# Key-weight sums on VectorE, queries in another buffer and quantised between later pairs, in a perceiver block

## What is computed

```python
q = (x @ Wq + bq).reshape(1, B * N, H, hd)
kv = (cond @ Wkv + bkv).reshape(1, -1, 2, H, hd)
k, v = (kv[:, :, 0], kv[:, :, 1])
scale = 1.0 / np.sqrt(hd).astype(np.float32)
q = jnp.transpose(q * scale, (0, 2, 1, 3))
...
q = _fq_sym(q, axis=-1)
k = _fq_sym(k, axis=-1)
v = _fq_sym(v, axis=2)
```

## Time and profile before

| | |
|---|---|
| median of 3 executions | 2779.63 us (2777.3 to 2780.09) |
| the profiled execution's own time | 2777.66 us |
| its span, first to last instruction | 2775.9 us |
| mean granted TensorE clock | 0.963 of 2.4 GHz |
| PE, DVE, ACT, POOL busy | 91%, 75%, 41%, 32% |
| stage A | from 0 to 92.3 us |
| stage B, pair 0 | 92.33 to 144.5 us |
| stage B, pairs 1 to 31 | from 144.51 us on, 38.86 us each where TensorE never waits |

### The profile page before, as it was taken

How to read it: one execution, slowest core, us unless ns; L and a number is a source line. 1 busy time by engine, 2 the same in 40 slices (tenths; PEclk the granted TensorE clock), 3 DMA queues, 4 the chain that set the end, 5 groups by cost and what they waited for, 6 DMA issues and landing times. The chain is left out here.

```text
span 2775.9 us, 42997 instructions
## 1 busy us (share of the span) xinstructions
PE 2525.2 (91%) x16296; PEld 1284.6 (46%) x16296; DVE 2084.2 (75%) x2967; ACT 1142.4 (41%) x1096; POOL 879.4 (32%) x385
## 2 busy tenths in 40 slices
PE   6699999999999999999878888888877999999998
PEld 3244444444444444444345454545554448544443
DVE  6877877778777877778679999999966434666664
ACT  3222222222222222222379999999982124311100
POOL 0432232223322233222256556466431460101100
PEclk9899999999999999999889999999998995899999
DMA  6043344433454345433668888888863223000000
GB/s 251 15 118 103 89 113 128 114 99 90 121 128 106 93 104 128 121 102 90 164 168 184 199 202 197 208 191 202 208 156 142 91 79 60 1 16 16 1 4 31
DMA packets 557343, 321.54 MB, mean 116 GB/s; under 512 B 401968, under 2 KB 533296, under 8 KB 552368
## 3 DMA queue, kind: packets, MB, share of 16 engines
q1 hardware_dynamic: 557232, 319.91, 44.7%
HBM read 149.95 MB, written 69.21 MB: 79 GB/s over the span
## 5 line engine op out<-in xcount | busy, mean ns | idle before, releaser
L1230 DVE TENSOR_SCALAR_CACHE_REDUCE at_sc<-at_score 128x1024 f32<-128x1024 f32 x512 | 601.6, 1219 | 21.0 <-PE at_score L1109 14.6
L1328 ACT ACTIVATE at_sc<-at_sc,at_bias,at_qs 128x4096 uint16<-128x4096 f32 x128 | 485.0, 3793 | 1.1 <-DVE at_bias L1242 1.1
L631 PE MATMUL kv_vacc<-kv_whi,kv_xthi 128*128 128x512 f16 x1024 | 388.9, 380 | 17.7 <-PEq L272 17.7
L631 PE MATMUL kv_vacc<-kv_wlo,kv_xthi 128*128 128x512 f16 x1024 | 388.9, 380 | 0.0
L631 PE MATMUL kv_vacc<-kv_whi,kv_xtlo 128*128 128x512 f16 x1024 | 388.9, 380 | 0.0
L639 PE MATMUL kv_kacc<-kv_wk,q_t 128*128 128x512 f16 x1536 | 347.0, 379 | 0.0
L712 ACT ACTIVATE q_t<-q_t 128x512 f16<-128x512 f32 x128 | 77.1, 626 | 503.1 <-POOL q_t L886 311.6
L884 POOL TENSOR_TENSOR q_t<-kv_rows 128x512 f32<-128x512 f32 x32 | 41.1, 1283 | 636.2 <-DMA kv_rows<-in_ctx 606.6
L639 PE MATMUL kv_kacc<-kv_wk,kv_xthi 128*128 128x512 f16 x768 | 229.5, 381 | 11.3 <-DVE kv_xtlo L490 11.3
L809 DVE SCALAR_TENSOR_TENSOR kv_val<-kv_vacc,kv_bias 128x512 f32<-128x512 f32 x128 | 87.7, 686 | 196.9 <-PE kv_vacc L631 193.1
L639 PEld LDWEIGHTS kv_kacc<-kv_wk,q_t 128*128 128x128 f16 x1536 | 150.3, 98 | 181.2
(11 more groups left out here) (228 smaller groups left out, 4329.3 us busy)
## 6 DMA issues: line engine op xcount, KB each, us to landing
kv_rows<-in_ctx SPq DMA_DIRECT2D x64, 512.0 KB, 7.0
values<-kv_val SPq DMA_DIRECT2D x32, 1024.0 KB, 6.4
keys_turned<-o SPq DMA_DIRECT2D x32, 1024.0 KB, 5.1
at_v_raw<-values SPq DMA_DIRECT2D x16, 2048.0 KB, 8.4
at_kt<-keys_turned SPq DMA_DIRECT2D x32, 512.0 KB, 5.2
x<-keys_turned SPq DMA_DIRECT2D x31, 512.0 KB, 5.2
x<-in_x SPq DMA_DIRECT2D x2, 2048.0 KB, 8.0
kv_wk<-in_wq SPq DMA_DIRECT2D x2, 2048.0 KB, 12.7
```

The costliest lines, as they stand in the source:

```text
L631: last = nc.tensor.matmul(v_acc[2 * s + c][:], a[s][:, k, :], b[:, c, k, :], start=(k == 0 and q == 0), stop=(k == KD - 1 and q == 2))
L1230: nc.vector.tensor_scalar(sc[n % 2][:, c * SC:(c + 1) * SC], score[pos % 2][:], 1.0, None, ALU.mult, ALU.max, accum_out=part_max[n % 2][:, ...
L1328: nc.scalar.activation(prob[n % 2][e], sc[n % 2][:, e * EC:(e + 1) * EC], ACT.Exp, bias=bias[n % 2][:], scale=qs_pair[j][:, t:t + 1], accu ...
```

## The change

Four things are altered; nothing else in the program is.

- The sums of the key weights move from GpSimd to VectorE, in stage A (`sums(dve, n)`, called three times), and the first sum t1 = b12 - b11 is written to a room of its own (`val`), so b11 stays whole. The table of the seven half-panels is in another order; products name them by new numbers. High parts 0 and 1 now wait for three low parts of panels, 2 and 3 for four. The low parts of the first pair's rows and the first two key weights stand ahead of the takes of the first Wq half.
- `x` and `o` are swapped: the queries lie in `x`, the raw key weights in `o`, which is free when the eight transposes are done. The bias of the queries has a tile of its own (`q_bias`).
- ScalarE splits the first Wq panel ahead of the transposed rows (`high_first=1`).
- Pair 0 nearly has the loop's order on TensorE: value(0,0) first, then M1, M6, M5, value(0,1), M7, M4, M2, M3, value(1,0), value(1,1). The queries are quantised between pairs: `queries.vector` behind pair 1, `queries.round` behind pair 2, the two ScalarE copies behind pairs 3 and 4. SyncE waits for them only after a quarter of the pairs.

```diff
             if ahead is not None:
-                kw.load(sp, turner.rows_ready, T * (turner.norms + 1))
+                kw.load(sp, turner.turned, turner.first + len(turner.units))
...
         def _(act):
+            turner.root(act)
+            for m in splits[:high_first]:
+                panels.high(act, m)
             turner.scalar(act)
-            for m in splits:
+            for m in splits[high_first:]:
                 panels.high(act, m)
...
             if ahead is not None:
-                act.wait_ge(panels.lo_ready, len(panels.sources))
-                for m in range(4):
-                    kw.high(act, m)
+                act.wait_ge(panels.lo_ready, 3)
+                kw.high(act, 0)
+                kw.high(act, 1)
+                act.wait_ge(panels.lo_ready, 4)
+                kw.high(act, 2)
+                kw.high(act, 3)
 
...
             turner.vector(dve)
             for m in split_first:
+                if ahead is not None and m == 2:
+                    kw.sums(dve, 0)
                 panels.low(dve, m)
+            if ahead is not None:
+                kw.low(dve, 0)
+                kw.sums(dve, 1)
+                kw.low(dve, 1)
+                kw.sums(dve, 2)
+                for s in range(2):
+                    tokens.low(dve, 0, s)
...
                 if ahead is not None and n == 0:
-                    for m in range(3):
-                        kw.low(dve, m)
-                    for s in range(2):
-                        tokens.low(dve, 0, s)
+                    kw.low(dve, 2)
                     kw.low(dve, 3)
...
-            if ahead is not None:
-                kw.sums(pool)
...
         act.wait_ge(self.scaled, 7)
-        for c in range(2):
-            self.nc.scalar.activation(self.twice[:, :, :, c, :], self.q[:].rearrange("p t (h d) -> p t h d", d=HD),
-                                      ACT.Copy).then_inc(self.step, 1)
+        self.nc.scalar.activation(self.twice[:, :, :, c, :], self.q[:].rearrange("p t (h d) -> p t h d", d=HD),
+                                  ACT.Copy).then_inc(self.step, 1)
...
+    def __init__(self, chip, wk, whole, key, val, wkv):
+        self.nc, self.wkv, self.whole = chip.nc, wkv, whole
...
+        t1 = val[:].rearrange("p h s d -> p (h s d)").rearrange("p (k n) -> p k n", n=HALF)
+        self.b11, self.b21, self.b12, self.b22, self.t1 = b11, b21, b12, b22, t1
+
+        self.raw = (b22, b21, b11, t1, b22, b12, b21)
...
-    def load(self, sp, rows_ready, n):
+    def load(self, sp, turned, n):
...
-        sp.wait_ge(rows_ready, n)
+        sp.wait_ge(turned, n)
         sp.dma_start(self.whole, self.wkv[0]).then_inc(self.loaded, 16)
...
         else:
-            act.wait_ge(self.summed, n - 2)
+            act.wait_ge(self.summed, (1, 3, 2, 4)[n - 3])
         if n == 6:
-            act.wait_ge(self.lo_ready, 5)
+            act.wait_ge(self.lo_ready, 6)
...
-    def sums(self, pool):
+    def sums(self, dve, n):
...
+        if n == 0:
+            dve.wait_ge(self.loaded, 48)
+            nc.vector.tensor_tensor(self.t1, self.b12, self.b11, ALU.subtract).then_inc(done, 1)
+            dve.wait_ge(done, 1)
+            nc.vector.tensor_tensor(self.b12, self.b22, self.b12, ALU.subtract).then_inc(done, 1)
+        elif n == 1:
+            dve.wait_ge(self.lo_ready, 1)
+            nc.vector.tensor_tensor(self.b22, self.b22, self.t1, ALU.subtract).then_inc(done, 1)
+        else:
+            dve.wait_ge(self.lo_ready, 2)
+            dve.wait_ge(done, 3)
+            nc.vector.tensor_tensor(self.b21, self.b21, self.b22, ALU.subtract).then_inc(done, 1)
...
-        q_room = queries.q[:].rearrange("p t n -> p (t n)").bitcast(F16)
+        q_room = room[:].rearrange("p t n -> p (t n)").bitcast(F16)
...
             body(0, True, False)
-            sp.wait_ge(queries.step, queries.DONE)
...
                     sp.wait_ge(k_stored, 16 * (n + 1) * quarter)
+                    if n == 0:
+                        sp.wait_ge(queries.step, queries.DONE)
                     heads.keys(sp, 0, 0, (n,))
...
                 pe.wait_ge(src.lo_ready, 2 * i + 1)
...
                 if first:
                     value_sums(i, first, 0, 0)
-                    value_sums(i, first, 0, 1)
-                    pe.wait_ge(src.lo_ready, 2)
-                    value_sums(i, first, 1, 0)
-                    value_sums(i, first, 1, 1)
-                if not first:
...
+                else:
                     pe.wait_ge(k_taken, 7 * (i - 1) + C11)
-                product(0, *low_half(0), 0)
+                product(0, *low_half(0), 2)
                 if not first:
...
                 else:
-                    pe.wait_ge(kw.lo_ready, 6)
+                    pe.wait_ge(kw.lo_ready, 5)
                 pe.wait_ge(s_lo_ready, 4 * i + 1)
-                product(1, *summed_rows(S2), 5)
+                product(1, *summed_rows(S2), 4)
                 if not first:
...
                 product(2, *summed_rows(S1), 3)
-                if not first:
-                    value_sums(i, first, 0, 0)
+                value_sums(i, first, 0, 1 if first else 0)
+                if first:
+                    pe.wait_ge(kw.lo_ready, 6)
                 pe.wait_ge(k_taken, 7 * i + U2)
...
-                product(1, *summed_rows(S3), 4)
+                product(1, *summed_rows(S3), 5)
                 pe.wait_ge(src.lo_ready, 2 * i + 2)
                 if first:
                     pe.wait_ge(kw.lo_ready, 7)
...
-                product(2, *summed_rows(S4), 2)
+                product(2, *summed_rows(S4), 0)
                 if not first:
                     value_sums(i, first, 0, 1)
-                    if last:
-                        for n in range(4):
...
-                    value_sums(i, first, 1, 1)
...
+                value_sums(i, first, 1, 0)
...
+                value_sums(i, first, 1, 1)
...
-                    act.wait_ge(kw.lo_ready, 6)
+                    act.wait_ge(kw.lo_ready, 5)
                 act.wait_ge(k_summed, 7 * i + M1)
                 nc.scalar.activation(key[:, 0, left], k_acc[0][:], ACT.Copy, scale=UNSCALE).then_inc(m1_ready, 1)
+                if first:
+                    kw.high(act, 6)
...
             sums_high(0, S1, None)
+            kw.high(act, 5)
             sums_high(0, S3, None)
             sums_high(0, S4, None)
-            kw.high(act, 5)
-            queries.scalar(act)
-            kw.high(act, 6)
-            each_pair(act, body)
+            body(0, True, False)
+            for i in range(1, 5):
+                body(i, False, False)
+                if i > 2:
+                    queries.scalar(act, i - 3)
+            with act.Fori(5, LAST_PAIR) as i:
+                body(i, False, False)
+            body(LAST_PAIR, False, True)
...
                     take_value(i, 0, 0)
-                    take_value(i, 0, 1)
                 else:
                     dve.wait_ge(v_stored, 16 * i)
...
-                if not first:
-                    take_value(i, 0, 1)
+                take_value(i, 0, 1)
                 low_parts(i, 1, 1)
...
-            queries.vector(dve)
-            queries.round(dve)
             kw.low(dve, 4)
             sums_low(0, S2)
             sums_low(0, S1)
+            kw.low(dve, 5)
             sums_low(0, S3)
-            kw.low(dve, 5)
-            each_pair(dve, body)
+            body(0, True, False)
+            body(1, False, False)
+            queries.vector(dve)
+            body(2, False, False)
+            queries.round(dve)
+            with dve.Fori(3, LAST_PAIR) as i:
+                body(i, False, False)
+            body(LAST_PAIR, False, True)
...
-                q = o
+                kw = KeyWeights(chip, wk, o[:].rearrange("p t n -> p (t n)").rearrange("p (k n) -> p k n", n=HALF), key, val,
+                                a["wkv"])
+                q = x
+                q_bias = chip.sb(c, "q_bias", [P, D], F32)
...
                 project(chip, "pq", panels, 0, 2, (0, 1, 2), ((3,), ()),
-                        (q, natural, xt_hi, xt_lo, ident32, x, None, x_loaded),
-                        lambda n, t: bias[:, cols(n)], lambda n, t: q[:, t, cols(n)], ahead=(kw, tokens))
+                        (o, natural, xt_hi, xt_lo, ident32, x, None, x_loaded),
+                        lambda n, t: bias[:, cols(n)], lambda n, t: q[:, t, cols(n)], ahead=(kw, tokens), high_first=1)
```

More of the change, by code:

```diff
@@ L259, in low, with project @@
                                             op1=ALU.subtract).then_inc(self.lo_ready, 1)
[L262 removed]
+def project(chip, tag, panels, first, count, split_first, split_after, rows, addend, out, added=None, beside=None, high_first=0,
             stats=None, ahead=None):
@@ L491, in low, with keys_and_values @@
                                             op0=ALU.mult, op1=ALU.subtract).then_inc(self.lo_ready, 1)
```

(3 more changed lines are left out.)

40 lines of the change are left out of this document (12 added, 28 removed).

## The result

| | before | changed |
|---|---|---|
| median | 2778.76 us (2777.3 to 2780.09, 4 runs) | **2762.74 us** (2760.14 to 2763.46, 4 runs) |
| span of the profiled execution | 2775.9 us | 2761.6 us |
| mean granted TensorE clock | 0.963 | 0.964 |

The ratio is 0.9942, 95% interval 0.993 to 0.9955: 16 us faster. The forecast was 2767, its range 2757 to 2773. The sign and the range held, and so did the gains of stage A and pair 0. The third term, what the moved queries cost, did not: TensorE waits 6.05 us in pairs 1 to 6 where the forecast had 13.6, which is under the 9 us that the forecast had named as a sign of being wrong. A smaller error, in the clock, hid part of that, and the median is 4.3 us from the forecast.

What follows compares the result with a forecast made beforehand. TensorE bounds the kernel from pair 1 on; only the way there can shorten. 25.4 us gained less 13.6 of waits is 11.8, giving 2765.9, plus about one for the median: 2767 us, range 2757 to 2773.

Steps and rivals of the forecast that it cites:

- the gains of stage A and pair 0: Ahead of pair 1: stage B begins 13.0 us earlier, pair 1 at 120.5 rather than 145.9, 25.4 us gained.
- The third term: Pairs 2 to 6: moved query steps delay M6's take and the row load, so TensorE waits 13.6 us.
- S: Stage A: time of one 128x2048 key-weight sum on VectorE, taken as 2.2 us, between 1.22 and 4.42.
- (c): Stage A gains less, by slower sums or late raw weights (+4.4 us): 2771 us; chance 0.11.
- (e): Stage A's end is set by something other than VectorE's chain, such as TensorE's end; chance with anything else 0.03.
- The ring: Each pair's cycle of row split, row load, row sums, low parts, quantising, next row split: 37.8 us a turn when late.
- (b): Pairs 2 and 3: only M6 itself is late, the load carries nothing on; net 20.8 us, 2758 us; chance 0.12.
- The clock behind the wait: Pairs 2 and 3: half-clock matmuls after two long waits cost little, since TensorE's next wait shrinks by as much.
- ScalarE's copies: Ahead of pairs 4 and 5: one query copy of 3.56 us each, 1.35 covered, 2.2 left, twice.
- (d): Pairs' loop: GpSimd meetings stretch a turn to 39.4 us, the lag never decays; slower, 2788 us; chance 0.04.

Runs made afterwards that it cites:

- e5: Changed kernel with ScalarE's split of the first Wq panel back behind the eight transposed parts (`high_first=0`): 2763.22 us.
- b1: Changed kernel with VectorE's query steps right behind M6's take in pairs 2 and 3, ScalarE's copies behind M1's copy in pairs 4 and 5: 2754.64 us.
- e3: Changed kernel with the four key-weight sums on GpSimd again, new order and room for t1 kept: 2766.27 us.
- b3: b2 with VectorE's split of the second value panel directly behind the first in stage A: 2748.37 us, ratio 0.9892 to the kernel before.
- b2: b1 with VectorE's query steps moved to pairs 4 and 5 and ScalarE's copies to pairs 6 and 7: 2752.76 us.

## Why the prediction was right, and which step was not

- **What bounds.** Right: the gain lies wholly ahead of pair 6, and the loop behind it runs as before.
- **Stage A.** Right to 0.2 us (79.09 against 79.3), and each term with it: S 2.29 for 2.2, splits 2.29 for 2.28, idle time of TensorE 5.91 for 5 to 7. VectorE's chain ends the stage: e5 moves TensorE's start by 2.6 us and the end by 0.5 (b1, with the stage as in the changed kernel, differs by 0.4 too), while e3 and b3 change which engine makes the sums or VectorE's order, and move the end by 4 us each. Rivals (c) and (e) fall.
- **Pair 0.** Right, 120.05 against 120.5, but by two numbers that don't fit together: I gave TensorE's own way to its end 1.9 us for the half clock, and VectorE's chain, which ended the pair in the sum, the same 1.9. In five other runs with stage B at 79 to 83 the pair takes 41.3 to 42.3 us, 40.96 in the changed kernel, and 39.43 at full clock in b3; so the half clock behind an idle stretch of 5 to 10 us costs 1.5 to 3 us. In each of these runs TensorE still waits 0.41 to 0.44 us for VectorE's row split at the end of the pair, so VectorE's chain, which takes TensorE's products, was stretched by as much.
- **The moved queries: the step that failed.** The pace that the takes of M6 showed before, "37.8 us a turn", was used as a constant. The ring without the moved steps takes 38.9, then 34.0, 34.0 and 36.0, because its load leg is 4.2 to 6.1 us and not 8 to 10 when VectorE comes late. Of the 13.6 us of waits 6.05 came, the first one about as forecast (5.62 for 5.1), the second not (0.18 for 5.1). The forecast had called itself wrong if the waits were under 9 us, and on this step it is. This is a delay that partly absorbs itself: the transfers that stood in the way had used the time to finish. Rival (b) had these waits at 3.6 + 1.0 and said that the load carries nothing on. At pair 6 the truth is nearer to it: the gain there is 17.8 us, where the forecast had 11.8 and (b) 20.8. The median lies midway, 4.3 us under the forecast and 4.7 over (b).
- **The clock behind the wait.** "Some matmuls at half clock behind the two long waits cost little, since TensorE's next wait for the ring shrinks by as much" failed too: there was no next wait to shrink, and the 1.5 us stayed. It took back part of the error above: 7.5 us less waiting, 2.0 more that is no waiting (1.5 of it in the slow row at 178.06), a pair 1 that is 0.5 earlier, and pair 6 stands 6.0 us ahead of the forecast. That the median is only 4.3 ahead, and inside the range, owes something to this error of the other sign.
- **ScalarE's copies.** Right in size (2.11 us of VectorE's waiting for 2.2, twice), wrong in effect: no wait of TensorE follows, since the ring already had the room.
- **(d), slower.** No sign of it: TensorE has no wait behind pair 6, and only the first turn is longer than forecast, by 1.1 us, with its long load leg. (Its time comes to 2787 by the forecast's own terms, not 2788.)

## What to carry to other kernels

A step that is moved into a loop costs by where in the pair it stands, not by how idle its engine is: the same 14 us of queries on VectorE (with their copies on ScalarE) cost about 8 us ahead of the step that reopens the loads, 2 to 3 us behind the take where VectorE waits for TensorE while the ring was late (b1), and nothing there once it had caught up (b2). Before the turn of a ring is multiplied, take it apart: here a leg made of transfers shrank when it was entered late, so not all of an engine's delay was passed on through it. And an order that lets ready work run ahead of waits can shorten a kernel twice, once by the wait and once by the TensorE clock that the wait would have cost, as in b3.
